# Three moves around a selective scan: drawn diagonals, quantization inside the scans, and a new order of preparation

## The chip, the cores and the metric

The kernel runs on one core of a Trainium2 chip. The metric is the device time of one execution in microseconds (us). Before the change three runs took 574.24, 575.33 and 576.14 us; their median is 575.33 us.

## What is computed

Two blocks with residual additions. `x` is 4 x 512 x 512 floats, `ctx` 4 x 512 x 256.

```python
# block 1: a state-space mixer over ctx (DI = 512 channels, DS = 16 states, L = 512 steps), gated by x
xc = causal_conv4(in_proj_w @ ctx)
u = silu(xc + conv_b)
dt_lo, Bm, Cm = split(x_proj_w @ u)
delta = softplus(dt_proj_w @ dt_lo + dt_proj_b)
for t in range(L):                       # for each channel and each of the 16 states
    state = state * exp(delta[t] * A) + (delta[t] * u[t]) * Bm[t]
    y[t] = sum over states of state * Cm[t]
x = x + (y + D * u) * silu(layernorm(x))
# block 2: a gated feed-forward layer (512 -> 2048 -> 512), activations rounded to 8 bits, weights to -1, 0, 1
def weight_quant(w):
    s = 1 / max(mean(|w|), 1e-5)
    return clip(round(w * s), -1, 1) / s
h = silu(q(ln(x)) @ wq(w_gate)) * (q(ln(x)) @ wq(w_up))
x = x + q(rms_norm(h) * ln_weight) @ wq(w_down)
```

## The kernel before

The program is written out engine by engine, each engine's list in an order set by hand, with semaphores between them. It has three stages.

**Preparation.** TensorE (PE) multiplies `ctx` by the input projection in eight units, `conv(b, h)` (batch b, half h of the channels); ACT applies the last convolution tap (`last_tap`), VectorE (DVE) adds the other three (`conv`), ACT applies silu (`silu_u`), PE projects (`project`, `turn_xdbl`, `delta_in`), ACT makes delta (`softplus`). GpSimd (POOL) multiplies delta by u (`du`), PE transposes that (`turn_du`) and DVE copies it out of PSUM (`keep_duT`) into `turned`. `x` is normalized: DVE takes the statistics (`x_stats`), POOL takes the power (`x_power`) and normalizes (`x_norm`, one `tensor_scalar` that subtracts the mean and multiplies), PE transposes (`turn_z`), ACT applies silu (`silu_z`). Between these stand the weights. `w_all` holds twelve pieces of 128 x 2048 floats: w_gate (w = 0), w_up (1), w_down (2), four each. All twelve are loaded and their absolute values summed here (`sum_weight`, on ACT or DVE; `total` on PE and `mean_weight` on DVE make the scale of each matrix). The eight pieces of w_gate and w_up are then scaled (`scale_weight`, ACT), cut to -1, 0, 1 (`cut_weight`, two DVE instructions or one of ACT) and stored to `w_ternary` in DRAM. The three units in PSUM that conv, dt, z and du share go round by `UNIT_USERS`.

**The scans.** 64 states k = 16 b + n. For each, ACT makes dA = exp(delta * A) in four instructions (128 x 512 each); DVE runs four scans (L929) over dA and a product dBu that PE makes in PSUM (`turn`); POOL multiplies the scans' result by the row C of the state (L475, `product`), which SP has loaded from `c_rows` in DRAM into one of two buffers (`load_c`, issued when the product two states earlier is done); PE adds that into y (`add`). There are two ways to dBu. For ten of sixteen n ACT scales the transposed du by B (L622, four of 128 x 512) and PE transposes it. For the six n in `DIAG = (1, 4, 6, 11, 13, 15)` ACT scales the identity by B instead (L619, four of 128 x 128), and PE multiplies the transposed du by this diagonal matrix. The ring for scan results, `hs`, has four slots, and dA has two: dA of state k waits for the scan of k - 2. After each batch DVE gates y (`gate_y`, L939) and POOL issues a load of x that adds onto it (`add_x`). The ternary weights come back from DRAM in the batches 1 and 2.

**The feed-forward part**, sixteen tiles of 128 rows, is paced by PE; w_down is scaled and cut on ACT here (L722, L729).

Of the kernel before, what the change touches and what calls it, by code (L numbers as in the profile page):

```python
# [68 lines left out]
def mixer_ffn(nc, x, ctx_t, in_t, conv_w, conv_b, xp_t, dt_t, dt_b, a_log, d_skip, w_all, ln_w, out):  # L69
    es = ExitStack()  # L70
    with es:
# [24 lines left out]
        du_s = part(128, 16).rearrange("p (s k l) -> p s k l", s=2, k=KE)  # L96
# [17 lines left out]
        c_bc = part(160, 4).rearrange("p (s l) -> p s l", s=2)  # L114
        skip = part(196, 2).rearrange("p (k e) -> p k e", k=KE)
# [4 lines left out]
        wg = part(0, 16).bitcast(BF16).rearrange("p (k n) -> p k n", k=4)  # L120
        wu = part(16, 16).bitcast(BF16).rearrange("p (k n) -> p k n", k=4)
# [34 lines left out]
        var_x, rstd_x = sb("var_x", [P, NB, KE]), sb("rstd_x", [P, NB, KE])  # L156
# [15 lines left out]
        def ps_end(half):  # L172
# [3 lines left out]
        wq_dram = nc.dram_tensor("w_ternary", [8, P, INNER], BF16).ap()  # L176
# [11 lines left out]
        c_loaded = [sem("c_loaded0"), sem("c_loaded1")]  # L188
        x_loaded = [sem(f"x_loaded{b}") for b in range(NB)]
# [21 lines left out]
        UNIT_USERS = (("conv", 0, 0), ("conv", 0, 1), ("conv", 1, 0), ("conv", 1, 1), ("conv", 2, 0), ("conv", 2, 1),  # L211
# [1161 lines left out]
```

## Time and profile before

| | us |
|---|---|
| median of three runs (lowest, highest) | 575.33 (574.24, 576.14) |
| span of the profiled execution | 572.7 |
| PE, DVE, ACT, POOL busy | 536.1, 535.1, 513.3, 465.1 |
| first scan starts | 93.42 |
| last scan ends | 393.50 |

For the profiled execution the page gives its span, from the first to the last instruction; the runs give the whole time. Their median lies 2.63 us above this span. The granted TensorE clock is 1.00 in nearly every slice. A busy share of over 90% on three engines is a mean over three stages that have different limits, so it has to be read stage by stage.

### The profile page before, as it was taken

Reading aid. Unit: us, or ns where it says so; the run is one execution under the profiler, and the core shown is the slowest. Engines: PE = TensorE matmul, PEld = TensorE weight load, DVE = VectorE, ACT = ScalarE, POOL = GpSimd, SP = SyncE. Lnnn points to the kernel's source line nnn. Section 1 sums busy time; section 2 is a strip of 40 time slices with the busy share of each in tenths; the row PEclk is TensorE's granted clock in tenths of the full one; section 3 lists DMA queues with packets and bytes.
Section 4 is the critical chain, followed back from the end, with each engine's and each line's share of the span. In section 5 each row is a group of like instructions: output and inputs, shape, how many; then the busy total and the mean of one; then the engine's idle time right before and its main releaser. Section 6 shows DMA issues by size and latency. Waiting matters only on the chain.

```text
span 572.7 us, 10285 instructions
## 1 busy us (share of the span) xinstructions
PE 536.1 (94%) x3667; PEld 403.2 (70%) x3684; DVE 535.1 (93%) x778; ACT 513.3 (90%) x757; POOL 465.1 (81%) x196
## 2 busy tenths in 40 slices
PE   5888988899999999999999889999899999999996
PEld 2335477799998999989899879998344444444443
DVE  3999988999999999999999999999999999999883
ACT  1899999999999999989999899999987878878784
POOL 4889364999999999999999999995757676675772
PEclk9999999999999999999999998999999999999999
DMA  9992591221111832126632257443544344533521
GB/s 279 408 390 76 201 323 36 55 58 57 56 56 56 191 105 93 56 65 123 165 99 63 59 129 188 137 154 97 83 78 96 76 101 84 110 84 71 106 55 74
DMA packets 62194, 68.64 MB, mean 120 GB/s; under 512 B 41137, under 2 KB 41137, under 8 KB 59969
## 3 DMA queue, kind: packets, MB, share of 16 engines
q1 hardware_dynamic: 59776, 63.59, 37.5%
q0 software_dynamic: 2368, 4.40, 4.8%
q8 instruction: 30, 0.49, 0.4%
q14 instruction: 20, 0.16, 0.1%
HBM read 50.02 MB, written 8.52 MB: 102 GB/s over the span
## 4 chain that ended last, share of the span: by engine, by line
PE 36%; ACT 24%; DVE 18%; POOL 9%; issue 7%; DMA 5%; SPq 0%; DVEq 0%; POOLq 0%
PE ps L1280 16%; ACT arena L697 11%; PE ps L1290 9%; POOL arena L475 9%; ACT arena L622 7%; DVE arena L840 5%; PE ps L1245 4%; PE ps L1229 4%; DMA arena<-c_rows 3%; DVE arena L929 3%; ACT arena L619 2%; PE ps L1232 2%; DVE bst_x L872 2%; DMA arena<-x 1%; DVE arena L864 1%
## 5 line engine op out<-in xcount | busy, mean ns | idle before, releaser
L475 POOL TENSOR_TENSOR arena<-arena 128x2048 f32<-128x2048 f32 x63 | 286.7, 4614 | 14.1 <-DVE arena L929 9.8
L929 DVE TENSOR_TENSOR_SCAN arena<-arena,ps 128x512 f32<-128x512 f32 x256 | 286.7, 1197 | 1.7 <-PE ps L1229 0.4
L697 ACT ACTIVATE arena<-arena,a_neg 128x512 f32<-128x512 f32 x256 | 164.8, 711 | 7.9 <-DVE arena L929 7.8
L1245 PE MATMUL ps<-ident,arena 128*128 128x128 f32 x1024 | 154.8, 274 | 5.9 <-POOL arena L475 3.7
L1245 PEld LDWEIGHTS ps<-ident,arena 128*128 128x128 f32 x1024 | 119.9, 141 | 9.7 <-POOL arena L475 5.3
L1280 PE MATMUL ps<-arena 128*128 128x512 bf16 x497 | 112.5, 379 | 3.6 <-DVE arena L1006 2.2
L1229 PE MATMUL ps<-arena 128*128 128x128 f32 x768 | 103.4, 278 | 3.9 <-DVE arena L929 3.8
L512 POOL TENSOR_TENSOR arena<-arena 128x1024 f32<-128x1024 f32 x30 | 71.0, 2366 | 39.9 <-DVE arena L1006 39.7
L622 ACT ACTIVATE arena<-arena,bT 128x512 f32<-128x512 f32 x160 | 102.0, 710 | 0.0
L1232 PE MATMUL ps<-ident,arena 128*128 128x128 f32 x640 | 96.0, 273 | 3.0 <-ACT arena L622 2.1
L1229 PEld LDWEIGHTS ps<-arena 128*128 128x128 f32 x768 | 94.5, 194 | 5.8 <-ACT arena L622 2.7
L1280 PEld LDWEIGHTS ps<-arena 128*128 128x128 bf16 x512 | 49.7, 98 | 63.6 <-DVE arena L1006 2.7
L1232 PEld LDWEIGHTS ps<-ident,arena 128*128 128x128 f32 x640 | 74.2, 141 | 5.6 <-issue 3.0
L1290 PE MATMUL ps<-arena 128*128 128x512 bf16 x254 | 57.6, 379 | 0.6 <-DVE arena L1079 0.3
L781 ACT ACTIVATE arena<-arena,magic,aq 128x2048 f32<-128x2048 f32 x14 | 29.3, 2095 | 21.9 <-DVE aq L970 21.9
L1290 PEld LDWEIGHTS ps<-arena 128*128 128x128 bf16 x256 | 24.9, 98 | 30.4 <-DVE arena L1079 0.5
L749 ACT ACTIVATE arena<-ps,scales 128x512 f32<-128x512 f32 x64 | 41.8, 678 | 4.0 <-PE ps L1280 3.1
L1006 DVE TENSOR_TENSOR arena<-arena,ps 128x512 f32<-128x512 f32 x64 | 43.5, 681 | 0.6 <-ACT arena L749 0.3
L1108 PE MATMUL ps<-arena 128*128 128x512 f32 x64 | 31.3, 640 | 8.9 <-DMA arena<-ctx_t 8.0
L993 DVE TENSOR_REDUCE half_max<-arena 128x1 f32<-128x1024 f32 x30 | 36.5, 1216 | 2.5 <-DVE var L954 0.5
L441 POOL TENSOR_SCALAR arena<-arena,mv_x,rstd_x 128x512 f32<-128x512 f32 x16 | 33.0, 2076 | 0.4
L840 DVE SCALAR_TENSOR_TENSOR arena<-ps,cw,arena 128x511 f32<-128x511 f32 (+2 forms) x48 | 31.8, 739 | 0.0
(122 smaller groups left out, 574.8 us busy)
## 6 DMA issues: line engine op xcount, KB each, us to landing
arena<-w_all SPq DMA_DIRECT2D x16, 1024.0 KB, 9.2
arena<-c_rows SPq DMA_DIRECT2D x64, 256.0 KB, 3.3
arena<-x SPq DMA_DIRECT2D x4, 1024.0 KB, 16.0
w_ternary<-arena SPq DMA_DIRECT2D x8, 512.0 KB, 4.1
arena<-w_ternary SPq DMA_DIRECT2D x8, 512.0 KB, 4.8
arena<-x POOLq DMA_DIRECT2D x4, 1024.0 KB, 10.6
out<-arena SPq DMA_DIRECT2D x16, 256.0 KB, 2.0
arena<-ctx_t SPq DMA_DIRECT2D x4, 512.0 KB, 14.0
```

The lines of the kernel that those rows point to most:

```text
L475: nc.gpsimd.tensor_tensor(hs[:, k % RING, :, :], hs[:, k % RING, :, :], c_bc[:, s:s + 1, :].to_broadcast([P, KE, L]), ALU.mult).then_inc(S ...
L512: nc.gpsimd.tensor_tensor(p2[:, s, w], h2[:, s, w], lnw[:, w], ALU.mult).then_inc(S["p2_ready"], 1)
L622: nc.scalar.activation(dB[:, slot(k), i, :], turned[:, b, i, :], ACT.Copy, scale=bT[:, b, i, n:n + 1]).then_inc(S["dB_ready"], 1)
L697: nc.scalar.activation(dA[:, s, i, :], delta_u[:, b, 0, i, :], ACT.Exp, scale=a_neg[:, i, n:n + 1]).then_inc(S["dA_ready"], 1)
L840: nc.vector.scalar_tensor_tensor(out=v[:, k, i:], in0=two("conv", b, h)[:, j, 0:L - i], scalar=cw[:, k, TAPS - 1 - i:TAPS - i], in1=v[:, k ...
L929: nc.vector.tensor_tensor_scan(out=hs[:, k % RING, i, :], data0=dA[:, k % 2, i, :], data1=ps[:, 4 + i, :], initial=0.0, op0=ALU.mult, op1= ...
L1006: nc.vector.tensor_tensor(h2[:, t % 2, j * 512:(j + 1) * 512], sg[:, j % 2, :], ps[:, U_BANK[(t * 4 + j) % 3], :], ALU.mult).then_inc(S["h ...
L1229: last = mm(to, turned[:, k // DS, c, i * P:(i + 1) * P], dgB[:, slot(k), c, :], start=True, stop=True)
L1232: last = nc.tensor.transpose(to, dB[:, slot(k), c, i * P:(i + 1) * P], ident[:])
L1245: last = mm(ps[:, c, i * P:(i + 1) * P], hs[:, k % RING, i, c * P:(c + 1) * P], ident[:], start=(n == 0 and i == 0), stop=(n == DS - 1), i ...
L1280: last = mm(ps[:, bank, :], q1T[:, t, c, :], w[:, c, j * 512:(j + 1) * 512], start=(c == 0), stop=(c == KE - 1))
L1290: last = mm(ps[:, DOWN_BANK[t % 2], :], q2T[:, t % 2, c, :], wd(c), start=(c == 0), stop=(c == KI - 1))
```

## The change

1. **Diagonals by DMA.** The 24 diagonal matrices no longer come from ACT. SP clears six blocks of `b_diagonals` in DRAM once, writes 512 single numbers of `bT` onto the diagonal of each (`draw_diag`) and loads 128 x 512 floats back into `dgB` (`load_diag`), two diagonal states ahead. PE waits for `dg_loaded`.
2. **w_down's sums and w_up's quantization in the scans.** In batch 1, ACT sums four pieces of w_down (after dA of the states 19, 22, 25, 28); in batches 2 and 3 it scales (states 33, 38, 43, 49) and cuts (each a state later) the four pieces of w_up, straight into `wu`. The eight loads for them, 1 MB each, are issued by ACT itself. w_up no longer goes through DRAM, and w_gate comes back in batch 2.
3. **Preparation in a new order.** All eight convs come first, batches interleaved; `x_stats(1)` to `(3)` follow. w_up is summed only, w_down isn't touched. One piece of w_gate is scaled on POOL, three on ACT; one is cut on ACT, three on DVE. `du(1)` and `du(3)` move from POOL to DVE.
4. **x normalized by add and multiply.** DVE also writes `minus_mean`; POOL's `tensor_scalar` adds it and multiplies. `skip` becomes multiply and add 0.

```diff
-        W_AT = ((128, 136, 144, 152), (64, 72, 80, 88), (96, 104, 96, 104))
+        W_AT = ((128, 136, 144, 152), (64, 72, 80, 88))
+        DOWN_STAGE, UP_STAGE = (64, 64, 64, 64), (64, 64, 64, 72)
+        DOWN_SUMMED, DOWN_TOTAL = {DS + 3: 0, DS + 6: 1, DS + 9: 2, DS + 12: 3}, 2 * DS + 4
+        UP_SCALED = {2 * DS + 1: 0, 2 * DS + 6: 1, 2 * DS + 11: 2, 3 * DS + 1: 3}
+        UP_CUT = {k + 1: n for k, n in UP_SCALED.items()}
...
+            def draw_diag(b, m):
+                if b > 0:
+                    sp.wait_ge(dg_loaded[m % 2], ((b - 1) * len(DIAG) + m) // 2 * 16 + 16)
...
+                    sp.dma_start(dg_diag(m), bT[:, b, :, DIAG[m]]).then_inc(dg_drawn[m], 16)
+            def load_diag(d):
+                k, m = d // len(DIAG) * DS + DIAG[d % len(DIAG)], d % len(DIAG)
+                hold(sp, "dBu_ready", slot_free(k))
+                sp.wait_ge(dg_drawn[m], (d // len(DIAG) + 1) * 16)
+                sp.dma_start(dgB[:, d % 2, :, :], dg_dram[m, :, :].rearrange("p (c l) -> p c l", c=KL)
+                             ).then_inc(dg_loaded[d % 2], 16)
...
-                    nc.gpsimd.tensor_scalar(row, row, mv_x[:, b, k, 0:1], rstd_x[:, b, k:k + 1], ALU.subtract,
+                    nc.gpsimd.tensor_scalar(row, row, minus_mean[:, b, k:k + 1], rstd_x[:, b, k:k + 1], ALU.add,
                                             ALU.mult).then_inc(S["x_normed"], 1)
...
+            def scale_weight(k):
+                pool.wait_ge(S["w_inv_ready"], 1)
+                nc.gpsimd.tensor_scalar(w_full(W_AT[0][k]), w_full(W_AT[0][k]), winv[:, 0:1], magic[:], ALU.mult,
+                                        ALU.add).then_inc(w_scaled[k], 1)
...
+            def load_stage(w, k):
+                stage = (UP_STAGE if w == 1 else DOWN_STAGE)[k]
+                nc.scalar.dma_start(w_full(stage), w_all[w * 4 + k, :, :]).then_inc(S["stage_loaded"], 16)
+            def sum_down(k):
+                act.wait_ge(S["stage_loaded"], (k + 1) * 16)
+                own.done(nc.scalar.activation(stage_junk, w_full(DOWN_STAGE[k]), ACT.Abs,
+                                              accum_out=wstat[:, 8 + k:9 + k]))
+            def cut_up(k):
+                act.wait_ge(S["w_scaled_act"], k + 1)
+                nc.scalar.activation(wu[:, k, :], w_full(UP_STAGE[k]), ACT.Sign,
+                                     bias=minus_magic[:]).then_inc(S["up_staged"], 1)
```

**DVE, the end of preparation.** Before, from its last conv to the first scan; L864 and L867 cut a piece of a weight, L847 sums one, L883 copies the turned du:

```order
L840 SCALAR_TENSOR_TENSOR arena<-ps,cw,arena 128x509 x2
L847 TENSOR_REDUCE wstat<-arena 128x1
L864 TENSOR_SCALAR arena<-arena 128x2x1024
L867 TENSOR_SCALAR arena<-arena 128x2x1024
L853 TENSOR_REDUCE wsum<-ps 128x1
```

After the change, from the second mean on; L988 is du(1) and du(3), L962 and L966 a cut, L984 a copy of the turned du, L1029 the scans:

```order
L988 TENSOR_TENSOR arena<-arena 128x2048
L984 COPY arena<-ps 128x1024
L962 TENSOR_SCALAR arena<-arena 128x2x1024
L966 TENSOR_SCALAR arena<-arena 128x2x1024
L984 COPY arena<-ps 128x1024
L962 TENSOR_SCALAR arena<-arena 128x2x1024
L966 TENSOR_SCALAR arena<-arena 128x2x1024
L984 COPY arena<-ps 128x1024 x2
L988 TENSOR_TENSOR arena<-arena 128x2048
L962 TENSOR_SCALAR arena<-arena 128x2x1024
L966 TENSOR_SCALAR arena<-arena 128x2x1024
L984 COPY arena<-ps 128x1024 x4
```

DVE had seven cuts and five sums of weights; now it has three cuts and two sums, and two multiplications of du.

**POOL, the preparation.** L502 is the normalization with add, L513 the scaling of one piece of w_gate, L507 du(0) and du(2), L536 the products of the scans:

```order
L496 TENSOR_TENSOR rstd_x<-var_x,mhalf 128x4
L519 TENSOR_SCALAR arena<-ident,dsk 128x128 x4
L502 TENSOR_SCALAR arena<-arena,minus_mean,rstd_x 128x512 x4
L513 TENSOR_SCALAR arena<-arena,winv,magic 128x2048
L496 TENSOR_TENSOR rstd_x<-var_x,mhalf 128x4
L502 TENSOR_SCALAR arena<-arena,minus_mean,rstd_x 128x512 x4
L507 TENSOR_TENSOR arena<-arena 128x2048
L496 TENSOR_TENSOR rstd_x<-var_x,mhalf 128x4 x2
L502 TENSOR_SCALAR arena<-arena,minus_mean,rstd_x 128x512 x8
L507 TENSOR_TENSOR arena<-arena 128x2048
L536 TENSOR_TENSOR arena<-arena 128x2048 x20
```

Three of the four normalizations now stand behind the first mean of the weights, where before all four began as soon as x had landed.

**ACT, in batches 1 and 2.** L657 sums a piece of w_down, L653 issues a load of 1 MB, L665 scales and L670 cuts a piece of w_up; L701 is dB and L775 dA:

```order
L775 ACTIVATE arena<-arena,a_neg 128x512 x4
L657 ACTIVATE arena,wstat<-arena 128x2048
L653 DMA arena<-w_all 128x2048
L701 ACTIVATE arena<-arena,bT 128x512 x4
L775 ACTIVATE arena<-arena,a_neg 128x512 x8
L701 ACTIVATE arena<-arena,bT 128x512 x4
L775 ACTIVATE arena<-arena,a_neg 128x512 x4
L665 ACTIVATE arena<-arena,magic,winv 128x2048
L775 ACTIVATE arena<-arena,a_neg 128x512 x4
L670 ACTIVATE arena<-arena,minus_magic 128x2048
```

The four identity scalings of a diagonal state are gone (hence dA x8), and whole 128 x 2048 instructions stand between dA and dB.

## Rows read from the trace of the kernel before

**Rows 1.** Busy time by stage: preparation, scans, the rest (length, then busy us).
```profile
0.00:93.42 93.42, 77.96 (x340) 44.52 (x340) 79.63 (x128) 77.22 (x78) 64.13 (x46) 1.00 0.73 262
93.42:393.50 300.08, 286.99 (x2515) 278.73 (x2513) 297.95 (x287) 291.67 (x514) 289.49 (x68) 0.99 0.36 98
393.50:572.70 179.20, 171.16 (x815) 79.99 (x832) 157.50 (x365) 144.38 (x167) 111.44 (x83) 1.00 0.39 82
```

The engines of a row are PE, PEld, DVE, ACT, POOL, with the number of instructions in brackets; then the granted clock, the DMA share and GB/s.

**Rows 2.** Chain of waits in preparation: shares by line; start us, us, what.
```profile
by line: DVE arena L840 33.8%; DVE bst_x L872 10.4%; DMA arena<-x 8.8%; DVE arena L864 7.6%; DVE wstat L847 7.1%; DMA w_ternary<-arena 5.1%; DVE arena L867 4.5%; ACT arena L569 3.0%; ACT arena L697 2.8%; ACT arena L622 2.6%; issue 2.0%; PE 
...
90.73 2.56 ACT arena L697 x4
```

**Rows 3.** Timeline of DVE up to the scans: start us, us.
```profile
10.98 2.47 DVE L872 BATCH_NORM_STATS2 bst_x<-arena 128x6 f32<-128x512 f32 x4 [8.12 <-DMA arena<-x]
...
13.98 7.96 DVE L840 SCALAR_TENSOR_TENSOR arena<-ps,cw,arena 128x511 f32<-128x511 f32 x12
...
24.85 7.96 DVE L840 SCALAR_TENSOR_TENSOR arena<-ps,cw,arena 128x511 f32<-128x511 f32 x12
...
61.26 1.22 DVE L864 TENSOR_SCALAR arena<-arena 128x2048 bf16<-128x2048 f32 x1
...
63.12 1.22 DVE L864 TENSOR_SCALAR arena<-arena 128x2048 bf16<-128x2048 f32 x1
...
64.98 4.47 DVE L847 TENSOR_REDUCE wstat<-arena 128x1 f32<-128x2048 f32 x2
...
84.11 2.35 DVE L883 COPY arena<-ps 128x1024 f32<-128x1024 f32 x2
...
93.42 82.40 DVE L929 TENSOR_TENSOR_SCAN arena<-arena,ps 128x512 f32<-128x512 f32 x74
```

**Rows 4.** The page's DMA rate, in 40 slices of the span (14.3 us each).
```profile
GB/s 279 408 390 76 201 323 36 55 58 57 56 56 56 191 105 93 56 65 123 165 99 63 59 129 188 137 154 97 83 78 96 76 101 84 110 84 71 106 55 74
```

**Rows 5.** Groups of instructions in preparation: count | busy us, mean ns | idle before.
```profile
L441 POOL TENSOR_SCALAR arena<-arena,mv_x,rstd_x 128x512 f32<-128x512 f32 x16 | 33.0, 2076 | 0.4
L1108 PE MATMUL ps<-arena 128*128 128x512 f32 x64 | 31.3, 640 | 8.9 <-DMA arena<-ctx_t 8.0 <-DVE arena L840 0.6
L451 POOL TENSOR_TENSOR arena<-arena 128x2048 f32<-128x2048 f32 x4 | 18.2, 4558 | 14.7 <-DVE arena L867 13.9 <-PE ps L1152 0.8
L581 ACT ACTIVATE arena<-arena,magic,winv 128x2048 f32<-128x2048 f32 x8 | 16.7, 2100 | 0.1
L574 ACT ACTIVATE arena<-arena 128x2048 bf16<-128x2048 f32 x7 | 13.4, 1909 | 1.0 <-DMA arena<-w_all 1.0
...
L464 POOL TENSOR_SCALAR arena<-ident,dsk 128x128 f32<-128x128 f32 x4 | 2.4, 609 | 0.0
```

**Rows 6.** Timelines of POOL and of DVE at the end of the scans: start us, us.
```profile
366.98 27.15 POOL L475 TENSOR_TENSOR arena<-arena 128x2048 f32<-128x2048 f32 x6 [0.59 <-DVE arena L929]
...
393.54 1.68 DVE L1026 TENSOR_TENSOR arena<-arena 128x1024 f32<-128x1024 f32 x1
```

**Rows 7.** DVE's multiplication of two SBUF inputs (L1026): ns min/median/max, starts.
```profile
L1026 DVE TENSOR_TENSOR arena<-arena x2: 1212/1444/1675, 393.5 to 395.1; 128x1024 f32<-128x1024 f32 x2
```

**Rows 8.** Timeline of ACT at the first states: start us, us.
```profile
93.19 1.26 ACT L619 ACTIVATE arena<-ident,bT 128x128 f32<-128x128 f32 x4
94.36 2.54 ACT L697 ACTIVATE arena<-arena,a_neg 128x512 f32<-128x512 f32 x4
96.81 2.54 ACT L622 ACTIVATE arena<-arena,bT 128x512 f32<-128x512 f32 x4
```

**Rows 9.** Timeline of POOL in the scans: start us, us [idle before].
```profile
98.11 81.49 POOL L475 TENSOR_TENSOR arena<-arena 128x2048 f32<-128x2048 f32 x18 [8.22 <-DVE arena L929]
```

**Rows 10.** Loads of C on SP's queue: issue ns min/median/max, and time to landing.
```profile
L333 SPq DMA_DIRECT2D arena<-c_rows x63: 319/319/1200, 82.8 to 385.1; - x63
...
DMA to landing us min/median/max: 3.0/3.3/6.0
```

**Rows 11.** Timeline of SP, the issue of a load of 512 single numbers.
```profile
2.25 0.51 SPq L264 DMA_DIRECT2D cb<-conv_b  x1
```

More of the change, by code:

```diff
@@ L188, in mixer_ffn @@
         c_loaded = [sem("c_loaded0"), sem("c_loaded1")]
+        dg_loaded = [sem("dg_loaded0"), sem("dg_loaded1")]
+        dg_drawn = [sem(f"dg_drawn{m}") for m in range(len(DIAG))]
         x_loaded = [sem(f"x_loaded{b}") for b in range(NB)]
@@ L562, in silu_u @@
             def silu_u(b):
-                act.wait_ge(S["conv_steps"], (b + 1) * 12)
+                hold(act, *both(unit_read, "conv", b))
                 u = flat(delta_u[:, b, 1])
@@ L692, in _ @@
                     s = k % 2
-                    if k > 0:
+                    if k in UP_SCALED:
+                        scale_up(UP_SCALED[k])
+                    if k in UP_CUT:
+                        cut_up(UP_CUT[k])
+                    if k > 0 and not is_diag(k):
                         inputs_of(k)
+                    if k < 2:
+                        hold(act, *both(unit_full, "du", 2 + k))
                     for i in range(KE):
@@ L831, in conv @@
                 v = delta_u[:, b, 1, :, :]
-                first = (b * 2 + h) * 6
+                first = ORDER["conv"].index((b, h)) * 6
                 for i in range(1, TAPS):
@@ L933, in scan @@
                         gate_y(k // DS - 1)
+                    if k == DOWN_TOTAL + 2 and i < 3:
+                        (add_total, mean_of, invert_mean)[i](2)
             def gate_y(b):
@@ L1095, in take @@
             def take(kind, b, h):
-                before = UNIT_USERS.index((kind, b, h)) - 3
-                if before >= 0:
-                    hold(pe, *unit_read(*UNIT_USERS[before]))
+                users = list(UNIT_AT)
+                before = [u for u in users[:users.index((kind, b, h))] if UNIT_AT[u] == UNIT_AT[kind, b, h]]
+                if before:
+                    hold(pe, *unit_read(*before[-1]))
                 return two(kind, b, h)
@@ L1166, in _ @@
             conv(0, 0)
+            conv(1, 0)
             conv(0, 1)
-            conv(1, 0)
+            conv(2, 0)
             conv(1, 1)
-            conv(2, 0)
+            conv(3, 0)
             conv(2, 1)
+            conv(3, 1)
+            pe.wait_ge(S["proj_loaded"], 16 * 6)
+            project(0)
+            delta_in(0, 0)
             pe.wait_ge(S["dve_consts"], 1)
             total(0)
-            conv(3, 0)
-            pe.wait_ge(S["proj_loaded"], 16 * 6)
-            project(0)
@@ L1177, in _ @@
-            conv(3, 1)
-            pe.wait_ge(S["w_mean_done"], 1)
+            delta_in(0, 1)
             pe.wait_ge(S["consts_set"], 3)
+            pe.wait_ge(S["w_added"], 1)
             turn_xdbl(0)
-            keep_warm(6)
-            delta_in(0, 0)
-            keep_warm(6)
             delta_in(1, 0)
-            keep_warm(6)
-            delta_in(0, 1)
+            project(1)
+            delta_in(1, 1)
+            delta_in(3, 0)
+            delta_in(3, 1)
+            delta_in(2, 0)
@@ L1225, in turn @@
                 hold(pe, "scan_done", (k - 1) * KE + i + 1)
+                if k == DOWN_TOTAL + 2 and i == KE - 1:
+                    total(2)
+                    pe.wait_ge(S["w_added"], 3)
                 for c in range(KL):
```

377 lines of the change are left out of this document (201 added, 176 removed), and 12 rows, old and new, of tables (ORDER, UNIT_AT, UNIT_USERS).

## The prediction

> **What bounds the kernel.** I read the busy time by stage first. The span of 572.7 us is 93.42 of preparation, 300.08 from the start of the first scan to the end of the last, and 179.20 of the rest [rows 1]. In the scans DVE is busy 297.95 of 300.08; ACT and POOL have 8 and 11 us to spare, PE 13. So the scans can become at most 2 us shorter, whatever ACT is relieved of: a gain has to come from an earlier first scan. The chain of waits says what sets that: nearly all of it is DVE (statistics, convolution taps, sums and cuts of weights), then a store of a ternary weight, and at last ACT with the first dA at 90.73 [rows 2]. The timeline of DVE shows that it has x at 10.98 and then works without a pause until the seventies [rows 3].
>
> **Preparation, DVE.** Durations from the rows, start to start where instructions follow each other. x_stats: 10.98 to 13.98, 3.0, plus 0.1 for the added minus_mean, x4 = 12.4. The conv units: 24.85 - 13.98 less one x_stats is 7.88 for two, so 3.94 x8 = 31.5. A cut: 63.12 - 61.26 = 1.86. A sum: 4.4 for two, 2.2. A copy of the turned du: 1.15 [rows 3]. The change takes away four cuts (7.4) and three sums (6.6), and moves one mean (0.5) into the scans. It adds du(1) and du(3), 128 x 2048 with both inputs in SBUF. The nearest row is half as long: 1.212 us for 1024 columns alone and 1.675 for the one that began at 393.54 beside POOL's last product, which ended at 394.13 [rows 6, 7]. So 2048 columns cost 2.4 alone; 4.5 each, the time of POOL's own product of that size, is my upper bound [rows 5]. I take 2.8. DVE's list is then 12.4 + 31.5 + two means 1.1 + two sums 4.4 + three cuts 5.6 + eight copies 9.2 + two du 5.6 = 69.8 us, and from 10.98 it ends at 80.8 if DVE never waits.
>
> It waits a little. I walked the new order with these durations and the loads landing at 400 GB/s, 2.6 us per MB, in their new order [rows 4]. PE makes a conv unit in under 4 us (31.3 for eight) and ends the eighth near 39 [rows 5]; the last tap of each reaches DVE in time, but for 0.2 us at the second. DVE ends the convs at 46 and has the first mean at 46.5; x(1), now the last of the first loads, lands near 44. The second mean waits for PE's total(1), behind project and five delta_in, until 61 (0.8). Then the first copy waits for du(0) of POOL and its transposition, 0.7. That makes 82.5 and, with an allowance for handovers, the first scan at **84.0** instead of 93.42: 9.4 less. Bounds: 82 (no contention) and 86 (4.5 for each du).
>
> **Who else could be late there.** ACT loses five scalings (2.0 each) and a sum (2.1), 12 us [rows 5], and would have dA(0) at 80, so it is covered by DVE. POOL is covered only if `tensor_scalar` becomes quicker. Now scaling w_gate's piece 0 waits for the first mean, 46.5, and behind it stand x_norm(1), du(0), x_norm(2), x_norm(3), du(2). Before, subtract and multiply on one input took 2.076 us for 512 columns, 4.05 ns a column, while a product of two inputs takes 4.558 for 2048, 2.2 ns [rows 5]. Multiply alone took 609 ns for 128 columns, the same slope [rows 5]. No row has add and multiply together. From both sides: at 1.1 ns (half of the product's rate, for one input instead of two) or at 2.2 POOL has du(2) at 73 or 77, and DVE remains the end of the chain; at 4.05 it is the first rival below. I take the fast side, since the two-input operation shows that the engine's loop can pass a column in 2.2 ns, and the slow row is of a form that the change leaves.
>
> The Trainium skill, "GPSIMD Engine Reference", section "Engine selection", calls one-input operations on this engine roughly line-rate; the row of L441, slower per column than the two-input product, contradicts it for subtract and multiply, and the page doesn't tell forms apart. By that rule scaling 2048 columns is an estimate of under 3 us, and the first scan stays at 84.
>
> The diagonals: bT of the first batches is ready near 60, the six draws and their loads follow. But SP's list has load_c(0) and load_diag(0) behind the store of w_gate's piece 1, which DVE cuts near 78. An issue takes 0.3 to 0.5 us and a load lands in 3.3 [rows 10, 11], so diagonal 0 is there near 85. State 1 needs it one state after the first scan, near 88. Hidden, with 3 us to spare; the bound is 0 to 3 late.
>
> **The scans.** A group of four dA or dB is 2.45 us from start to start, an identity group 1.17 [rows 8]. A batch cost ACT 10 x 4.90 + 6 x 3.62 = 70.7; without the identities 63.7. DVE needs 82.4 / 74 = 1.113 us a scan [rows 3], 71.2 a batch, and 73.6 with a gate. Batch 0: ACT gets ahead, but dA's two slots let it lead by two states at most; DVE keeps its pace, gain 0. Batch 1: four sums, 2.3 each with their read and the wait for themselves, and five DMA issues on ACT, 0.4 to 0.5 each as on SP [rows 11]: 63.7 + 9.2 + 2.2 = 75.1 against 73.6. Batch 2: three scalings and three cuts at 2.05 and three issues: 63.7 + 12.3 + 1.3 = 77.3 against 73.6, and DVE has another 0.5 for w_down's mean. Batch 3: 63.7 + 4.1 + the old 4 is less than DVE's 78. So ACT is short by 5 us over batches 1 and 2, against a lead of 5 to 7 us which it can store only until each next burst. Walking the states with these numbers, the lead is used up around states 26 and 44 (a sum or a cut just before a state with dB), and DVE stalls 1 to 2 us at each. I also expect POOL to wait for C a few more times: C normally lands in 3.3 of the 4.52 us that a product leaves, (81.49 for 18), and the slowest took 6.0 [rows 9, 10]; eight loads of 1 MB on ACT's queue now run beside them, where eight of 0.5 MB ran before. In all **+4** for the scans (bounds -2, all of DVE's pauses gone, and +9, all of ACT's deficit and 4 us of waits for C).
>
> The Trainium skill, "DMA: Bandwidth & Descriptors", section "Issuing engines are not separate DMA queues", says that DMAs of all queues run on the same 16 engines and interleave. The late landings in the batches with weight loads agree (6.0 at the most, 3.3 in the median). By it the loads on ACT's queue delay C as much as on SP's, which is the upper bound's last term.
>
> **The rest** is unchanged in order and loads: 0. PE's wait for w_down's mean falls into state 38, where 1.3 us of PE stand against scans already fed; 0.
>
> **Sum**: 572.7 - 9.4 + 4.0 = 567.3 of span; with the 2.6 that lie between the span before and the median of its runs, 569.9. I predict **570 us**, 0.9% faster.
>
> **Rivals.**
> A. *Add and multiply is no faster on POOL.* Scaling 46.5 to 54.6, x_norm(1) to 64.0, du(0) to 68.5, two powers to 70.8, eight rows of x_norm 16.6 to 87.4, du(2) to 91.9; then its transposition, two copies and more on DVE: first scan 97.5, 4.1 later than before, and with the +4 of the scans 583 us. For it: both one-input rows lie at 4 ns whatever the second operation is. Against it: the product's 2.2 ns. It decides from about 3.1 ns a column, where the first scan comes near 89.4 and the gain is just eaten by the scans. This one is slower than before.
> B. *The scans take back all that preparation gives*: ACT's bursts stall DVE in six or more places, and C's landings starve POOL, +8 to +10: 574 to 576. For it: three engines are busy over 96% there [rows 1], so nothing catches up. Against: batch 0 and batch 3 have room.
> C. *The scans cost nothing*: lead and ring absorb everything, 84.0 or 82.5 and +0: 564.5 to 566.
> D. *The diagonals come late*: small writes land later than my 3.3 us, each late diagonal holds PE, and so a part of 24 states; at 0.3 us each +7: 577. Their loads are issued four or more states ahead, which speaks against it.
>
> **Chances.** Forecast (566 to 573) 0.60; C 0.08; B and a middling POOL rate together 0.12; D 0.04; A 0.16. A measurement of this kernel can tell about 0.3%, 1.7 us, from no change. Faster: forecast, C and a part of B, 0.71. Same: the rest of B, 0.08. Slower: A, D and a tail, 0.21. The range from 563.5 to 580 leaves out A and little else. The forecast's own range is 566 to 573.
>
> **What would show it.** First scan at 82 to 86; POOL's normalization of 512 columns under 1.2 us; DVE without an idle stretch over 1 us before the scans; scan stage 302 to 306, with DVE's new idle time ended by ACT's dA around states 26 and 44; ACT's DMA issues 0.4 us each. Wrong: a normalization near 2 us, du on DVE over 4, or the first scan held by a diagonal.

## The result and the profile after

The changed kernel takes **576.27 us** (median of 20 runs, 574.23 to 577.64), the kernel before on the same chip 574.42 us. The ratio is 1.0028, with a 95% interval of 1.0020 to 1.0037: slower by 0.3%, just measurable. The forecast was 570, faster. The profiled execution took 577.64 us, 2.0 above its span of 575.6 and 1.4 above the median: it is the slowest of the twenty, so the three stages below are together 1.4 us longer than in the median execution.

Busy time by stage, with the columns of [rows 1]:

```profile
0.00:87.49 87.49, 71.69 (x284) 38.00 (x284) 77.96 (x122) 67.77 (x74) 39.12 (x45) 1.00 0.63 224
87.49:395.60 308.11, 290.82 (x2515) 283.60 (x2514) 298.85 (x290) 288.75 (x432) 289.07 (x68) 0.98 0.47 137
395.60:575.60 180.00, 171.36 (x815) 79.84 (x832) 158.10 (x364) 143.85 (x166) 111.98 (x83) 1.00 0.39 82
```

The first scan starts at 87.49 instead of 93.42: 5.9 us won. The scans last 308.11 instead of 300.08: 8.0 lost. DVE has nearly the same work in both (298.85 and 297.95 us), so its idle time there went from 2.1 to 9.3 us. The rest is 0.8 longer, which is its scatter: with the same program in it, it lasts 179.2 to 180.8 in the runs below.

Preparation, DVE (start us, us, instruction, and in brackets the idle time before it with its releaser), to be compared with [rows 3]:

```profile
45.84 0.16 DVE L942 TENSOR_REDUCE wsum<-ps 128x1 f32<-128x4 f32 x1
...
56.65 3.40 DVE L976 TENSOR_SCALAR minus_mean<-mv_x 128x4 f32<-128x4 f32 x1
...
63.56 2.29 DVE L988 TENSOR_TENSOR arena<-arena 128x2048 f32<-128x2048 f32 x1
...
66.90 1.42 DVE L962 TENSOR_SCALAR arena<-arena 128x2048 bf16<-128x2048 f32 x1
68.35 1.16 DVE L966 TENSOR_SCALAR arena<-arena 128x2048 bf16<-128x2048 bf16 x1
...
75.33 5.85 DVE L988 TENSOR_TENSOR arena<-arena 128x2048 f32<-128x2048 f32 x1
81.10 1.21 DVE L962 TENSOR_SCALAR arena<-arena 128x2048 bf16<-128x2048 f32 x1
82.35 0.69 DVE L966 TENSOR_SCALAR arena<-arena 128x2048 bf16<-128x2048 bf16 x1
...
93.37 3.70 DVE L1029 TENSOR_TENSOR_SCAN arena<-arena,ps 128x512 f32<-128x512 f32 x3 [0.23 <-PE ps L1329]
```

and POOL in the same stretch:

```profile
46.48 2.05 POOL L513 TENSOR_SCALAR arena<-arena,winv,magic 128x2048 f32<-128x2048 f32 x1 [26.92 <-DVE winv L952]
...
50.65 3.01 POOL L502 TENSOR_SCALAR arena<-arena,minus_mean,rstd_x 128x512 f32<-128x512 f32 x4
55.49 4.53 POOL L507 TENSOR_TENSOR arena<-arena 128x2048 f32<-128x2048 f32 x1 [1.83 <-ACT arena L685]
...
64.44 10.09 POOL L502 TENSOR_SCALAR arena<-arena,minus_mean,rstd_x 128x512 f32<-128x512 f32 x8
74.50 4.53 POOL L507 TENSOR_TENSOR arena<-arena 128x2048 f32<-128x2048 f32 x1
```

Read the two together. From 19 us to the first scan DVE has no idle stretch over 0.1 us, so a list of waits shows nothing; what grew is the length of single instructions. Minus_mean on four numbers takes 3.40 us, and it ends when POOL's du(0) ends (55.49 + 4.53 = 60.02; 56.65 + 3.40 = 60.05). du(3) takes 5.85; POOL's du(2) ends at 79.03, and from there it is 2.15 to du(3)'s end, close to the 2.24 that one takes alone (e4). There is one exception: du(1) began at 63.56 beside POOL's power of 128 x 4, which ran from 63.33 to 64.34, and with 2.29 it shows no wait. The two cuts beside POOL's x_norm take 1.42 and 1.16 each, the last one, alone, 1.21 and 0.69. POOL pays too: eight rows of x_norm take 10.09 where four alone take 3.01.

In the scans, DVE stands at these places (timeline of DVE):

```profile
204.35 1.22 DVE L1029 TENSOR_TENSOR_SCAN arena<-arena,ps 128x512 f32<-128x512 f32 x1 [1.55 <-PE ps L1332]
206.48 1.22 DVE L1029 TENSOR_TENSOR_SCAN arena<-arena,ps 128x512 f32<-128x512 f32 x1 [0.91 <-PE ps L1332]
...
284.14 1.22 DVE L1029 TENSOR_TENSOR_SCAN arena<-arena,ps 128x512 f32<-128x512 f32 x1 [3.31 <-PE ps L1332]
285.93 6.78 DVE L1029 TENSOR_TENSOR_SCAN arena<-arena,ps 128x512 f32<-128x512 f32 x6 [0.56 <-PE ps L1332]
```

These are the states 25 and 41; the trace names PE. PE's list goes by turns: one of the four parts of dBu of a state, then one part of the addition of the product three states earlier. PE in turn waited for POOL, and POOL for C (timeline of POOL; L544 is the issue of the accumulating load of x, L536 the products):

```profile
184.18 1.38 POOL L544 DMA_DIRECT2D arena<-x  x1
...
197.95 18.09 POOL L536 TENSOR_TENSOR arena<-arena 128x2048 f32<-128x2048 f32 x4 [3.26 <-DMA arena<-c_rows]
...
262.56 1.21 POOL L544 DMA_DIRECT2D arena<-x  x1
263.38 9.48 POOL L536 TENSOR_TENSOR arena<-arena 128x2048 f32<-128x2048 f32 x2
277.14 13.58 POOL L536 TENSOR_TENSOR arena<-arena 128x2048 f32<-128x2048 f32 x3 [4.27 <-DMA arena<-c_rows]
```

C for state 22 was issued at 190.18 and landed 7.7 us later, C for state 38 at 268.38 and landed 8.7 later; before, these two took 6.0 and 5.7 of a median of 3.3 [rows 10]. PE makes the first part of dBu of state 25 (41), then stands before the addition of state 22 (38) until that late product is there, and DVE stands before the second scan. So it is PE's order that stops DVE, and not the ring hs, which the expectation of e1 below names: the first scan of state 25 has its slot already. What was under way around C for state 38 (transfers issued from 264 to 279 us: count, KB, median us to landing):

```profile
arena<-w_all ACTq DMA_DIRECT2D x1, 1024.0 KB, 9.9
arena<-c_rows SPq DMA_DIRECT2D x2, 256.0 KB, 7.9
arena<-w_ternary SPq DMA_DIRECT2D x1, 512.0 KB, 9.6
arena<-b_diagonals SPq DMA_DIRECT2D x1, 256.0 KB, 9.1
```

Beside these runs the load of x, issued at 262.56 and landed at 277.31.

A part of the lost time is TensorE's clock. In the scans of the kernel before it falls once, near 345 us; in the changed kernel it falls there and at three more places. Here they are (stretch, PE busy, and before the DMA share and GB/s the granted clock; 0.50 is 1.2 instead of 2.4 GHz):

```profile
90.80:94.00 3.20, 3.20 (x17) 0.50 0.00 0
203.40:206.70 3.30, 3.30 (x18) 0.50 0.76 223
282.00:285.20 3.20, 3.20 (x17) 0.50 0.59 154
```

Up to 0.8 us before each of them began, PE had stood still, 2.57 us for diagonal 0, 2.42 and 3.54 us for the late product. Then it is slow just when DVE waits for it (timeline of PE, the same four additions at either clock; then the 32 matmuls of state 1, in the changed kernel and, at full clock, in e1):

```profile
283.81 1.06 PE L1345 MATMUL ps<-ident,arena 128*128 128x128 f32 x4
285.63 0.60 PE L1345 MATMUL ps<-ident,arena 128*128 128x128 f32 x4
```

```profile
90.06 5.46 PE L1329 MATMUL ps<-arena 128*128 128x128 f32 x32 [2.57 <-DMA arena<-b_diagonals]
```

```profile
90.22 3.84 PE L1330 MATMUL ps<-arena 128*128 128x128 f32 x32 [1.26 <-DMA arena<-b_diagonals]
```

The smaller gaps of DVE stand in these stretches: 0.91 and 0.15 at state 25, 0.56 at state 41, 0.23 and 0.15 at state 1. Together 2.0 us of the 8.0 that the scans lost.

One part of the change stands in its diff, but not in its four points. The kernel before has seven calls of `keep_warm` between PE's transpositions in preparation, 27 matmuls of ones by ones whose result nobody reads. The changed kernel has none. No run puts them back, so it is not shown whether the clock at state 1 would stay up with them.

### The profile page after: what moved, and what is told of

Its sections match the earlier page's. It is cut to its first block, busy times and chain, and to the rows that moved or that the text cites. A ratio compares the mean times of both kernels' runs of the same rounds, so it can differ in the third digit from the quotient of the medians.

```text
span 575.6 us, 10175 instructions
## 1 busy us (share of the span) xinstructions
PE 533.9 (93%) x3613; PEld 401.4 (70%) x3630; DVE 534.9 (93%) x774; ACT 500.4 (87%) x670; POOL 440.2 (76%) x195
## 4 chain that ended last, share of the span: by engine, by line
PE 46%; DVE 21%; issue 12%; POOL 11%; ACT 5%; DMA 5%; SPq 1%; DVEq 0%; POOLq 0%; ACTq 0%
PE ps L1380 13%; POOL arena L536 10%; PE ps L1345 9%; PE ps L1390 8%; PE ps L1329 8%; PE ps L1332 6%; DVE arena L930 5%; DVE arena L1029 4%; DMA arena<-w_all 2%; PE ps L1357 2%; ACT arena L775 2%; ACT arena L701 1%; DVE bst_x L971 1%; DVE arena L988 1%; DVE arena L1108 1%
## 5 line engine op out<-in xcount | busy, mean ns | idle before, releaser
L536 POOL TENSOR_TENSOR arena<-arena 128x2048 f32<-128x2048 f32 x63 | 286.9, 4599 | 27.5 <-DVE arena L1029 16.5
L1029 DVE TENSOR_TENSOR_SCAN arena<-arena,ps 128x512 f32<-128x512 f32 x256 | 287.5, 1197 | 8.8 <-PE ps L1332 6.5
L775 ACT ACTIVATE arena<-arena,a_neg 128x512 f32<-128x512 f32 x256 | 166.1, 711 | 18.7 <-DVE arena L1029 15.3
L1345 PEld LDWEIGHTS ps<-ident,arena 128*128 128x128 f32 x1024 | 122.0, 143 | 13.2 <-POOL arena L536 8.2
L701 ACT ACTIVATE arena<-arena,bT 128x512 f32<-128x512 f32 x160 | 102.0, 709 | 1.0 <-PE ps L1332 0.5
L1329 PEld LDWEIGHTS ps<-arena 128*128 128x128 f32 x768 | 95.6, 196 | 7.2 <-issue 3.9
L1332 PEld LDWEIGHTS ps<-ident,arena 128*128 128x128 f32 x640 | 75.3, 142 | 4.5 <-issue 4.3
L1211 PEld LDWEIGHTS ps<-arena 128*128 128x128 f32 x64 | 13.0, 207 | 24.7 <-issue 21.6
```

The lines of the kernel that those rows point to most:

```text
L536: nc.gpsimd.tensor_tensor(hs[:, k % RING, :, :], hs[:, k % RING, :, :], c_bc[:, s:s + 1, :].to_broadcast([P, KE, L]), ALU.mult).then_inc(S ...
L701: nc.scalar.activation(dB[:, slot(k), i, :], turned[:, b, i, :], ACT.Copy, scale=bT[:, b, i, n:n + 1]).then_inc(S["dB_ready"], 1)
L775: nc.scalar.activation(dA[:, s, i, :], delta_u[:, b, 0, i, :], ACT.Exp, scale=a_neg[:, i, n:n + 1]).then_inc(S["dA_ready"], 1)
L1029: nc.vector.tensor_tensor_scan(out=hs[:, k % RING, i, :], data0=dA[:, k % 2, i, :], data1=ps[:, 4 + i, :], initial=0.0, op0=ALU.mult, op1= ...
L1329: last = mm(to, turned[:, k // DS, c, i * P:(i + 1) * P], dgB[:, slot(k), c, :], start=True, stop=True)
L1332: last = nc.tensor.transpose(to, dB[:, slot(k), c, i * P:(i + 1) * P], ident[:])
```

## The experiments

Ratios are to the kernel before, run beside each (medians of 574.75 to 575.69 us); unless another kernel is named, the experiment is the changed kernel with one edit. The changed kernel itself wasn't run beside them again: differences to it are to its 576.27 us. Span, first scan and length of the scans are of the profiled execution, which in e11 and e12 is the slowest of its runs (576.77 and 588.02 us).

### e1: the weight loads moved

The loads of 1 MB that ACT issues no longer stand at its states 19 to 23 and 35 to 41, around the loads of x.

```diff
-        DOWN_SUMMED, DOWN_TOTAL = {DS + 3: 0, DS + 6: 1, DS + 9: 2, DS + 12: 3}, 2 * DS + 4
-        UP_SCALED = {2 * DS + 1: 0, 2 * DS + 6: 1, 2 * DS + 11: 2, 3 * DS + 1: 3}
+        DOWN_SUMMED, DOWN_TOTAL = {DS + 2: 0, DS + 8: 1, DS + 11: 2, DS + 14: 3}, 2 * DS + 4
+        UP_SCALED = {2 * DS + 1: 0, 2 * DS + 6: 1, 2 * DS + 13: 2, 3 * DS + 1: 3}
+        UP_LOADED = {2 * DS + 2: 1, 2 * DS + 10: 2, 2 * DS + 14: 3}
```

> The changed kernel with the same work, but the loads of 1 MB that ACT issues, and the sums, scalings and cuts that need them, moved by a few states, so that no such load is issued while x is being added onto the gated rows (issued after the states 18, 24, 27, 30 and 34, 42, 46 instead of 19, 22, 25, 28 and 34, 39, 44). Theory C (rows of C land late where a 1 MB load meets the accumulating load of x, POOL starves, and DVE stalls at the states 25 and 41 on a full ring): the landings of C at the states 22 and 38 fall from 7.7 and 8.7 us to 6 or less, the stalls of 2.9 and 4.1 us go, scans 308 to 302, device time 576.3 to 570 or 571. Theory A (ACT's added work is too much for batches 1 and 2): the stalls move with the bursts, time stays at 576 within 1 us.

Measured: 571.19 us, ratio 0.9944 (0.9929 to 0.9959), 5.1 below the changed kernel. Same work, same bytes, another time of issue. The scan stage:

```profile
87.28:388.70 301.42, 288.68 (x2523) 280.13 (x2521) 298.09 (x290) 287.49 (x432) 289.35 (x68) 0.99 0.50 140
```

301.42 instead of 308.11. C for the states 22 and 38 lands in 5.1 and 5.6, and the gaps at 25 and 41 are gone, the clock stays at 1.00 there. State 1 loses nothing either: 0.6 of the 6.7 us is that. A new gap of 1.4 us stands at state 34, where dA is 0.2 us ahead. The same view of transfers, 264 to 279 us:

```profile
arena<-w_ternary SPq DMA_DIRECT2D x2, 512.0 KB, 6.1
arena<-w_all ACTq DMA_DIRECT2D x1, 1024.0 KB, 6.6
arena<-c_rows SPq DMA_DIRECT2D x3, 256.0 KB, 4.6
arena<-b_diagonals SPq DMA_DIRECT2D x1, 256.0 KB, 5.4
```

### e2: small weight loads

It leaves out 31/32 of the staged weights.

```diff
-                nc.scalar.dma_start(w_full(stage), w_all[w * 4 + k, :, :])
+                nc.scalar.dma_start(w_full(stage)[:, 0:64], w_all[w * 4 + k, :, 0:64])
```

> The changed kernel, but each of the eight loads that ACT issues in the scans brings only the first 64 of 2048 columns (w_down's sums and w_up's ternary values are then of other numbers; every instruction of ACT, DVE, PE and POOL has its old size). Theory C: without this traffic C lands in 6 us at the most, as before the change, the stalls at 25 and 41 go, scans about 301 to 302, device time 569 to 570. Theory A: ACT's work is unchanged, so the time stays at 576 within 1 us.

Measured: 571.73 us, ratio 0.9958 (0.9943 to 0.9973); scans 302.52. C for the states 22 and 38 takes 6.2 and 5.8 us. ACT does the same work as in the changed kernel, and 5.6 us of the scans are gone, 0.6 of them at state 1: the transfers, not ACT's work, cost the other 5.0. It stays above what the theory wanted, and why shows in the timeline of DVE:

```profile
206.97 4.55 DVE L1029 TENSOR_TENSOR_SCAN arena<-arena,ps 128x512 f32<-128x512 f32 x4 [1.54 <-PE ps L1332]
```

This is state 26: dA for it is ready at 206.74, 0.2 us before the scan starts, and the same happens at state 44 (a gap of 1.2). Those are the two states where the prediction had ACT short.

### e9: small x loads

The other one of the two large transfers is taken away.

```diff
-                nc.gpsimd.dma_start(gate_rows(b), x_v[:, b, :, :], accum_op=ALU.add)
+                nc.gpsimd.dma_start(gate_rows(b)[:, :, 0:32], x_v[:, b, :, 0:32], accum_op=ALU.add)
```

> The changed kernel, but the accumulating load of x after each batch brings 32 of 512 columns (it leaves the rest of x out of the sum); the loads of weights stay as they are. If it is the meeting of two large loads that delays C, taking away the other one of the two does the same as small weight loads did: C for the states 22 and 38 lands in under 6 us, the scans take 302 to 303.5, and the time is 571 to 572.5. Rival: the weight loads of 1 MB delay C by themselves, whatever runs beside them: then C for 22 and 38 still takes 7 us or more and the time stays at 575 or above.

Measured: 573.10 us, ratio 0.9968 (0.9951 to 0.9986); scans 303.40. C for the states 22 and 38 takes 4.0 and 5.3 us, as the theory of a meeting wants, with the weight loads at full size. So neither of the two delays C that far by itself. The time is 0.6 above the forecast, and DVE again stands for ACT at the states 26 and 44 (timeline of DVE):

```profile
207.30 1.22 DVE L1029 TENSOR_TENSOR_SCAN arena<-arena,ps 128x512 f32<-128x512 f32 x1 [1.58 <-PE ps L1332]
...
293.86 6.78 DVE L1029 TENSOR_TENSOR_SCAN arena<-arena,ps 128x512 f32<-128x512 f32 x6 [0.93 <-PE ps L1332]
```

At state 26 two more gaps follow, 0.59 and 0.82 us, which e2 doesn't have: there the granted clock is 0.50 from 207.4 to 210.7, after PE had stood 2.17 us for ACT.

### e4: du(0) and du(2) on DVE

```diff
-            du(0)
...
-            du(2)
...
             x_stats(3)
+            du(0)
             mean_weight(1)
             du(1)
...
+            du(2)
             du(3)
```

The two lines go from POOL's list and come into DVE's.

> The changed kernel with all four multiplications of du on DVE (du(0) before the second mean, du(2) before du(3)), none on POOL. Theory P (DVE and POOL block each other when both read two SBUF inputs or DVE is in a fast copy mode: the minus_mean of 128x4 took 3.40 us, du(3) 5.85 beside POOL where du(1) alone took 2.29): minus_mean back to 0.17, each du about 2.3, DVE saves 3.3 + 3.6 and pays 4.6, first scan from 87.5 to 85 or 86, device time 574 to 575. Rival (these were waits for something else, and POOL was only near by): the long instructions stay, first scan at 91 to 92, device time 580.

Measured: 574.40 us, ratio 0.9994 (0.9977 to 1.0010), 1.9 below the changed kernel, whose interval (1.0020 to 1.0037) it doesn't touch; first scan 85.05, scans 307.68. DVE's end of preparation with du on it twice more:

```profile
56.62 0.17 DVE L974 TENSOR_SCALAR minus_mean<-mv_x 128x4 f32<-128x4 f32 x1
...
59.83 2.28 DVE L986 TENSOR_TENSOR arena<-arena 128x2048 f32<-128x2048 f32 x1
...
74.26 4.48 DVE L986 TENSOR_TENSOR arena<-arena 128x2048 f32<-128x2048 f32 x2
```

DVE has 4.5 us more to do and is ready 2.4 us sooner. Minus_mean is back at 0.17, and du(2) and du(3) take 2.24 each. What POOL's two products cost DVE was more than the products themselves. POOL can be the one that waits: its power of 128 x 4, which takes 1.01, took 2.91 beside DVE's du(0).

### e3: the kernel before, x normalized by add and multiply

```diff
-nc.gpsimd.tensor_scalar(row, row, mv_x[:, b, k, 0:1], rstd_x[:, b, k:k + 1], ALU.subtract,
+nc.gpsimd.tensor_scalar(row, row, minus_mean[:, b, k:k + 1], rstd_x[:, b, k:k + 1], ALU.add,
```

> The kernel before with one part of the change alone: x is normalized by adding minus_mean and multiplying (DVE writes minus_mean as well). If POOL's normalization was nowhere on the path: 512 columns take 0.75 instead of 2.08 us, DVE has four more instructions of 0.1 us, device time as before within 0.3%. Rival (POOL, idle sooner, starts du earlier or meets DVE's two-input instructions less): first scan 1 to 2 us earlier, 0.3% faster.

Measured: 575.09 us, ratio 1.0007 (0.9994 to 1.0020); first scan 93.38. As expected, the fourth part brings nothing without the third.

### e12: subtract again

The changed kernel with the same line turned back (the minus and plus of e3 change places).

> The changed kernel, but POOL normalizes x by subtract and multiply as before, in the new order of preparation. It prices the prediction's first rival: at 2.08 us for 512 columns the eight rows of the second x_norm take 16.6 instead of 10.1 us (6 to 6.5 more), the first 4 more, and du(2) ends near 91; first scan 95 to 98, the time 584 to 587 with the scans as in the changed kernel. If the pair of operations didn't matter, nothing would change: 576.

Measured: 585.03 us, ratio 1.0185 (1.0161 to 1.0209); first scan 98.24, scans 306.97. POOL's timeline:

```profile
50.70 8.24 POOL L502 TENSOR_SCALAR arena<-arena,mv_x,rstd_x 128x512 f32<-128x512 f32 x4
58.92 4.54 POOL L507 TENSOR_TENSOR arena<-arena 128x2048 f32<-128x2048 f32 x1
...
67.27 19.99 POOL L502 TENSOR_SCALAR arena<-arena,mv_x,rstd_x 128x512 f32<-128x512 f32 x8
87.23 4.51 POOL L507 TENSOR_TENSOR arena<-arena 128x2048 f32<-128x2048 f32 x1
```

du(2) ends at 91.74. In the new order the fourth part is worth 8.8 us: it is what lets the third part gain at all. A little of the late first scan is the clock, 0.50 from 76.3 to 93.3 in this execution, in which PE starts to transpose du(2) and du(3). With subtract, the scalar also comes from another tile (`mv_x` instead of `minus_mean`); no run separates that from the operation.

### e8 and e11: the kernel before with the diagonals alone

The first part of the change is put into the kernel before. In e8 the draws stand ahead of three stores of ternary weights, in e11 behind all of them and behind two loads of C:

```diff
-            for m in range(len(DIAG)):
-                draw_diag(0, m)
             store_weight(1, 1)
...
             load_c(1)
+            for m in range(len(DIAG)):
+                draw_diag(0, m)
             load_diag(0)
```

> The kernel before with the first part of the change alone: diagonals drawn and loaded by DMA, ACT relieved of 28 us in the scans. Theory: DVE is busy 298 of 300 us there, so nothing is gained, and the diagonal loads cost C little while no loads of 1 MB run beside them: 573.5 to 575.5, the same as before. Rival one (late diagonals hold PE in the scans): 577 or more. Rival two (ACT was a hidden bound of the scans): 572 or less.

> As the run with the diagonals alone, but the six draws stand behind all stores of ternary weights and the first two loads of C on SP's list. In that run the scans took 300.07 us as before and only the first scan was late, by 1.64 us: the draws held the store of w_up's piece 1 from 74.7 to 82.7, and a copy on DVE waits for it. If that is all, the first scan is back at 93.4 and the time at 574.5 to 576, the same as before. Rival: the traffic of the draws itself delays preparation, wherever they stand: 577 or more.

Measured: e8 577.91 us, ratio 1.0043 (1.0029 to 1.0056), scans 300.07, first scan 95.06; e11 575.70 us, ratio 1.0005 (0.9993 to 1.0018), scans 299.83, first scan 94.55. In both the scans are as long as before, so the diagonals' traffic costs them nothing, and relieving ACT brings nothing either. What e8 lost lies in preparation. One cause is SP's queue:

```profile
74.72 7.89 SPq L311 DMA_DIRECT2D b_diagonals<-bT  x6
82.66 2.11 SPq L301 DMA_DIRECT2D w_ternary<-arena  x3
```

Six draws hold the queue for 7.89 us, and a copy of DVE at 86.38 waits 1.75 us for the store behind them. In e11 that wait is gone and the time is that of before, yet the first scan of its profiled execution is still 1.1 late, so two thirds of e8's delay remain with the draws behind the stores. They come from TensorE's clock: from 80 to 84 us it is 1.00 in the kernel before, 0.58 in e8 and 0.62 in e11. The 16 transpositions of a z take (before, then e11)

```profile
80.51 1.91 PE L1142 MATMUL ps<-ident,arena 128*128 128x128 f32 x16
```

```profile
80.56 3.24 PE L1186 MATMUL ps<-ident,arena 128*128 128x128 f32 x16
```

and ACT's silu of it begins at 83.84 instead of 82.46, the first dA at 92.12 instead of 90.73. In e11 the draws are issued from 84.84 on, after the clock fell; why it fell in these two executions stays open.

### e7: identities on ACT

The first part of the change is undone, all else stays.

```diff
-                    if k > 0 and not is_diag(k):
+                    if k > 0:
                         inputs_of(k)
...
+                    if is_diag(k):
+                        nc.scalar.activation(dgB[:, slot(k), i, :], ident[:], ACT.Copy,
+                                             scale=bT[:, b, i, n:n + 1]).then_inc(S["dB_ready"], 1)
```

> The changed kernel without its first part: the 24 identity matrices are scaled on ACT again, nothing else is undone. If drawing them by DMA is what makes room for w_down's sums and w_up's quantization, ACT gets 24 x 1.17 = 28 us back in a stage where it is busy 288.8 of 308.1: ACT becomes the bound, the scans take 314 to 322, and the time is 582 to 590. Rival: the new DMA traffic of the diagonals is what delays C, and ACT's slack is enough: then C for the states 22 and 38 lands under 6 us and the time is under 575.

Measured: 582.93 us, ratio 1.0139 (1.0122 to 1.0155); the scan stage:

```profile
87.28:400.81 313.53, 290.47 (x2523) 279.96 (x2521) 300.13 (x290) 309.98 (x524) 288.99 (x68) 0.99 0.39 114
```

ACT is busy 309.98 of 313.53: it is the bound. The first part gives 6.7 us here and nothing in e11; it only pays for the second part. C for the states 22 and 38 still takes 7.7 and 7.6 us, with no diagonals under way, so their loads aren't what makes C late.

### e5: three mends together

e1's table, e4's lists, and the first two diagonals loaded one store earlier:

```diff
             store_weight(3)
+            load_diag(0)
+            load_diag(1)
             store_weight(1)
```

> The changed kernel with three mends together: the weight loads moved away from the accumulating load of x (as in the run with the loads moved), du(0) and du(2) on DVE (as in that run), and the first two diagonals loaded before the last ternary weight is stored. If the costs are separate, the first scan starts at 85.0 (the run with du on DVE) and the scans take 301.4 (the run with the loads moved), less 0.5 for the first diagonal: span 566.3, time 568.5. Rival: the two gains are one (an earlier first scan is eaten by ACT, which in the run with the loads moved has only 0.2 us of lead at state 34): then 571, as with the loads moved alone.

Measured: **568.53 us**, ratio 0.9883 (0.9867 to 0.9898), the fastest of all; first scan 85.27, span 565.6. Scans and rest:

```profile
85.27:386.36 301.09, 288.17 (x2515) 280.37 (x2514) 298.45 (x290) 287.67 (x433) 289.39 (x68) 0.99 0.48 138
386.36:565.60 179.24, 171.18 (x815) 79.91 (x832) 157.78 (x365) 143.73 (x166) 111.58 (x83) 1.00 0.38 82
```

The gains add up: 5.1 and 1.9 alone, 7.7 together with the earlier diagonals.

### e6 and e10: ACT's work spread out

e6 is e5 with w_up's first two scalings later, and so its second load at state 39. e10 has the same scalings, but two buffers by turns, so that this load can go out at state 35.

```diff
-        UP_SCALED = {2 * DS + 1: 0, 2 * DS + 6: 1, 2 * DS + 13: 2, 3 * DS + 1: 3}
-        UP_LOADED = {2 * DS + 2: 1, 2 * DS + 10: 2, 2 * DS + 14: 3}
+        UP_SCALED = {2 * DS + 3: 0, 2 * DS + 9: 1, 2 * DS + 13: 2, 3 * DS + 1: 3}
+        UP_LOADED = {2 * DS + 7: 1, 2 * DS + 11: 2, 2 * DS + 14: 3}    # e6
+        UP_LOADED = {2 * DS + 3: 1, 2 * DS + 10: 2, 2 * DS + 14: 3}    # e10, UP_STAGE = (64, 72, 64, 72)
```

> As the run with three mends, but w_up's first two scalings and cuts two and three states later (35, 36 and 41, 42 instead of 33, 34 and 38, 39), their loads at 39, 43 and 46. Theory: in the run with the loads moved DVE stood 1.8 us at state 34 since ACT had a sum, a scaling and a cut within five states; spread out, ACT keeps a lead there and the scans lose 1.5 us more: 567. Rival: that stall is PE's own at the batch's border, or it only moves to a later state: no difference from three mends.

> As the run with three mends, but the stage for w_up has two buffers by turns, so that its second load can be issued at state 35, ahead of the accumulating load of x, and its scalings and cuts stand at 35/36 and 41/42 as in the balanced run. Theory: the balanced run lost 4.5 us because its second load, issued at state 39, ran into the load of x (C for state 38 took 8.64 us); with the load early that goes, and ACT no longer stops DVE at state 34: span 565, time 567.5. Rival: ACT's order is worth nothing, or the early load delays C at 36 to 38 all the same: 568.5 or more.

Measured: e6 572.61 us, ratio 0.9946 (0.9928 to 0.9964), a miss; e10 569.02 us, ratio 0.9897 (0.9879 to 0.9915), not to be told from e5. e6 put a load of 1 MB beside the load of x again: C for state 38 took 8.6 us, DVE stood 3.3 us at state 41 (PE at half clock there too, from 275.9 to 279.2), and the scans took 305.48. With the load early (e10), C for 38 takes 5.1 and the scans 301.32. DVE's idle time in the states 33 and 34 went from 0.5 us to 0.2, and 0.5 came at state 42, where dA is 0.2 us ahead: spreading ACT's work moved its stall.

## Why the prediction was wrong

By its own terms: first scan 84.0, measured 87.49 (+3.5); scans +4, measured +8.0 (+4.0); the rest 0, measured +0.8; 2.6 from span to time, measured 0.7 from that span to the median (-1.9). Together 6.4 above the 569.9 of the sum. Of the last term, 1.4 is that the profiled execution is slower than the median one.

**The step that failed for the sign: the scans.** The prediction named ACT as the cause of +4 and made C a few short waits more, with a bound of 4 us on them. It was C, and behind it PE, which the prediction had 13 us to spare and whose clock it put at nothing. Of the 8.0 us, 4.9 are DVE's first gaps at the states 25 and 41, which end with the late product, 2.0 the gaps at half clock, 0.9 more work of DVE. The prediction did say that the loads of weights run beside those of C, but priced them by the slowest landing of before (6.0) and never laid the load of x, issued by POOL at each batch's border, and the new table of ACT's loads over each other. Two loads of 1 MB under way together make 256 KB late by 4 to 5 us, at two places, and e1, e2, e9 and, by accident, e6 show it from both sides: 6.7, 5.6 and 4.7 us of the scans go when either is moved or made small (0.6 of each at state 1, where no such load is under way), 4.4 come back over e5 when they meet.

**ACT's shortage was real but covered.** In the changed kernel ACT's dA was never less than 1.5 us ahead, and no stall at 26 or 44 was ACT's. But with C's delay gone DVE stands there for ACT, at just these states (e2, e9). The two waits stand behind each other: while POOL's lateness holds DVE at 25 and 41, ACT gets its lead back. Their prices don't add up; the later one counts. So rival B came nearest, with its size and the C half of its mechanism; the stalls of ACT in six or more places, its other half, didn't come.

**The step that failed in preparation: du on DVE and who is beside it.** The walk was right until 46 (45.84), and du(1) took 2.29 for the 2.8 taken. Then minus_mean cost 3.2 more, du(3) 3.1 above the 2.8, and two cuts beside x_norm about 1.4: 7.7, against which stand 0.5 at du(1) and 3.2 of waits and handovers in the sum that never came, since DVE was always the later one. That leaves 4.0, where 3.5 were measured. (The starting point was also read too strongly: DVE's five entries in the chain of [rows 2] make 63%, not nearly all of it.) The upper bound of 4.5 was too low, since a DVE instruction can cost its own time and the rest of POOL's instruction as well. The row for it stood in the prediction: 1.675 us for the product that began 0.59 before POOL's last one ended, where 1.212 is its own time [rows 6, 7]. It was read as a slower rate instead of a wait; waiting and own time would make 1.80 there, so the row fits it only roughly. The Trainium skill says this in "SBUF — State Buffer", section "Who interferes with whom": a DVE instruction with two inputs in SBUF, or a `tensor_scalar` in a two-port mode, and a GpSimd instruction that reads SBUF exclude each other, and the loser waits for the whole instruction. The trace agrees for these two: minus_mean ends with POOL's du(0), du(3) 2.15 us after POOL's du(2). It doesn't for du(1) beside the small power.

**POOL's rate was right, and rival A's price nearly.** Four rows of 512 columns take 3.01 us, 0.75 each against 2.08 before; e12 gave 98.24 and 585.0 for the 97.5 and 583 of that rival. The first number is its mechanism, the second partly luck: the scans lost 6.9 us instead of 4, and the median lies 1.0 below the span of the profiled execution instead of 2.6 above. **Diagonals:** 90.0 instead of 85, since they stand behind a store that DVE's delay held up; state 1 lost 0.6 us, within the bound of 0 to 3. But the late landing alone doesn't cost it: in e1 diagonal 0 lands at 90.2, as late after the first scan, PE makes state 1 at full clock, and DVE has no gap. It is the half clock from 90.7 to 94.1 that makes 3.84 us of PE's work 5.46. Rival D did not come. **The rest** and **ACT's issues** (0.33 us each) were near enough.

## What to carry to other kernels

Before a load is put into a stage that is paced by small loads, write down every transfer under way in each stretch, of all queues, and keep two large ones apart; the same bytes cost 4 to 6 us or next to nothing. Look at the granted clock wherever PE has just waited: an engine with 13 us to spare cost 2 here, because it was slow just when the others needed it. When work moves from one engine to another beside GpSimd, price it as its own time plus what is left of GpSimd's instruction, and look for the price in the length of instructions, not in idle time. And a part of a change that gains nothing alone (the diagonals, the normalization) may be what another part lives on: judge it by taking it out as well as by putting it in.

## What the runs showed that was not expected

- A `tensor_scalar` on GpSimd that subtracts and multiplies takes 2.08 us for 512 columns, one that adds and multiplies 0.75, and multiply and add 2.05 for 2048 columns. For 512 columns that is a factor of nearly three. With the operand unchanged, `skip` (128 columns) went from 0.61 us for multiply alone to 0.36 for multiply and add 0.
- A diagonal that lands 2.5 to 2.9 us after the first scan costs nothing at full TensorE clock and 0.6 us at half (e1, changed kernel).
- A DVE instruction on 128 x 4 numbers took 3.40 us beside GpSimd's product and 0.17 without it.
- Moving 4.5 us of work onto the engine that bounds preparation made preparation 2.4 us shorter (e4).
- Six strided writes of 512 single numbers held SP's queue for 7.9 us in e8.
